# One VectorE addition in place of eight TensorE transposes in every group of a sparse attention layer

## What is computed

```
q, k, v = z @ Wq + bq, z @ Wk + bk, z @ Wv + bv
scores  = einsum('ehd,ehd->eh', q[row], k[col]) * scale + bias
p       = exp(scores - segment_max(scores, row)[row])
out     = segment_sum((p / ssum[row])[:, :, None] * v[col], row)
```

## Time and profile before

| | |
|---|---|
| time, median of 3 runs | 3586.26 us (3585.55 to 3590.37) |
| profiled execution, first to last instruction | 3582.9 us |
| PE busy | 2804.5 us (78%), 18837 instructions |
| VectorE busy | 2651.1 us (74%), 6486 instructions |
| ScalarE busy | 1708.3 us (48%) |
| GpSimd busy | 2364.8 us (66%) |
| mean granted clock of TensorE | 0.878 |

### The profile page before, as it was taken

One profiled execution on the slowest core, in us unless ns is written; L12 is line 12 of the kernel. 1 busy time (PEld: TensorE's weight loads), 2 busy tenths in 40 slices (PEclk: granted clock), 3 DMA queues, 4 the chain that ended last, 5 costly groups with the idle time before them and its releaser, 6 DMA issues.

```text
span 3582.9 us, 83361 instructions
## 1 busy us (share of the span) xinstructions
PE 2804.5 (78%) x18837; PEld 2141.8 (60%) x18838; DVE 2651.1 (74%) x6486; ACT 1708.3 (48%) x6613; POOL 2364.8 (66%) x2567
## 2 busy tenths in 40 slices
PE   8666566666656666388889988989899999999987
PEld 7433333333333333377777777778777877777775
DVE  9776676776766677377787877778777777787775
ACT  0111111111111111277777677777777767677774
POOL 0477777777777777676766666666666666666660
PEclk9877766667766677699999999999999999999999
DMA  7323322223332322777888888788788787878760
GB/s 293 84 81 84 85 77 80 75 79 79 88 81 75 82 75 72 281 286 273 293 300 302 280 298 310 275 296 301 258 295 286 275 293 269 304 271 304 245 220 24
DMA packets 287973, 719.27 MB, mean 201 GB/s; under 512 B 89203, under 2 KB 105779, under 8 KB 287686
## 3 DMA queue, kind: packets, MB, share of 16 engines
q0 software_dynamic: 214080, 585.55, 47.0%
q1 hardware_dynamic: 73862, 133.41, 11.9%
HBM read 725.41 MB, written 72.97 MB: 223 GB/s over the span
## 4 chain that ended last, share of the span: by engine, by line
PE 23%; issue 20%; POOL 19%; DVE 16%; DMA 7%; DVEq 6%; ACT 5%; ACTq 1%; POOLq 1%; SPq 0%; PEld 0%; PEldq 0%
POOL records L411 18%; PE bank L1358 9%; DMA records<-region_c,pos_i 6%; ACT region_c L731 5%; DVE region_c L1021 4%; PE wide L1417 3%; PE bank L1401 3%; PE bank L1258 2%; PE wide L1428 2%; PE wide L1376 2%; DVE region_c L1032 2%; POOL region_a L535 2%; DMA region_a<-kv,cols 1%; PE wide L1386 1%; DVEq L1056 1%
## 5 line engine op out<-in xcount | busy, mean ns | idle before, releaser
L535 POOL DMA_INDIRECT region_a<-kv,cols x1176 | 1174.0, 998 | 532.6 <-issue 454.6
L411 POOL DMA_INDIRECT records<-region_c,pos_i x1024 | 1012.7, 989 | 445.1 <-issue 410.6
L731 ACT ACTIVATE region_c<-region_a,pr 128x64 f32 x4704 | 1171.2, 336 | 33.7 <-issue 33.7
L1021 DVE TENSOR_TENSOR region_c<-region_a,bank 128x1024 f32<-128x1024 f32 x588 | 678.9, 1214 | 68.1 <-issue 48.1
L1358 PE MATMUL bank<-ident,region_c 128*128 128x128 f32 x4704 | 596.2, 281 | 115.6 <-DVE region_c L1021 112.3
L1358 PEld LDWEIGHTS bank<-ident,region_c 128*128 128x128 f32 x4704 | 568.3, 195 | 150.8 <-issue 145.6
L1376 PE MATMUL wide<-ident,region_c 128*128 128x128 f32 x4704 | 574.7, 275 | 78.7 <-ACT region_c L731 78.7
L1376 PEld LDWEIGHTS wide<-ident,region_c 128*128 128x128 f32 x4704 | 521.5, 144 | 113.0 <-ACT region_c L731 113.0
L653 ACT COPY region_c<-region_a 128x64 f32 x128 | 32.5, 254 | 1066.1 <-DMA records<-region_c,pos_i 1066.1
L1316 PE MATMUL bank<-region_b,region_a 128*128 128x512 f32 x768 | 493.6, 802 | 0.0
L1032 DVE TENSOR_TENSOR region_c<-region_a,bank 128x1024 f32<-128x1024 f32 x294 | 344.3, 1211 | 0.5 <-issue 0.5
(11 more groups left out here) (185 smaller groups left out, 3206.8 us busy)
## 6 DMA issues: line engine op xcount, KB each, us to landing
region_a<-srcT SPq DMA_DIRECT2D x128, 256.0 KB
region_a<-kv,cols POOLq DMA_INDIRECT x1176, 5.9
region_a<-hiT SPq DMA_DIRECT2D x256, 64.0 KB
records<-region_c,pos_i POOLq DMA_INDIRECT x1024
x_rows<-region_c SPq DMA_DIRECT2D x32, 512.0 KB, 3.4
kv<-region_a SPq DMA_DIRECT2D x32, 512.0 KB
records<-region_c SPq DMA_DIRECT2D x32, 480.0 KB, 14.8
region_a<-in_x_dram SPq DMA_DIRECT2D x32, 256.0 KB, 3.2
```

The costliest lines, as they stand in the source:

```text
L411: pool.indirect_dma_start(records, bass.IndirectOffsetOnAxis(ap=pos_i[j % 2][:, s:s + 1], axis=0), rec_w[j % 2][:, s, :], None).then_inc(S ...
L535: pool.indirect_dma_start(KV[r][:, s, :], None, kv, bass.IndirectOffsetOnAxis(ap=cols[r][:, s:s + 1], axis=0), bounds_check=L - 1, oob_is_ ...
L731: last = act.activation(vw[:, s, of], v_part[:, s, C + hd * D:C + (hd + 1) * D], ACT.Copy, scale=pr[:, s + 1, hd:hd + 1])
L1021: last = dve.tensor_tensor(prods[:, of, :], kv_in[:, of, 0:C], q_ps[:, :].unsqueeze(1).broadcast_to([P, 2, C]), ALU.mult)
```

## The change

VectorE weighs its pairs in the other order, slots 4-5 first, waits for its pipeline to empty (`drain`), and adds the second pair onto the first: `vw[2:4] = vw[2:4] + vw[4:6]`, 128 by 1024 floats, both inputs and the output in SBUF. A new semaphore `v_added` tells TensorE that the sum is there; `sum_v(1)` waits for it, `sum_v(2)` is dropped, and six slots are transposed and accumulated in place of eight. The slots of GpSimd's ring are still released by the two multiplications.

```diff
-                for s in range(2, GROUP - 2, 2):
-                    dve.wait_ge(SUMMED[s // 2], groups)
+                for s in (4, 2):
+                    if s == 2:
+                        dve.wait_ge(SUMMED[1], groups)
                     dve.tensor_tensor(vw[:, s:s + 2, :].rearrange("p s (h d) -> p s h d", h=HEADS),
...
                                       ALU.mult).then_inc(V_READY[s // 2], 1)
+                dve.drain()
+                dve.tensor_tensor(vw[:, 2:4, :], vw[:, 2:4, :], vw[:, 4:6, :], ALU.add).then_inc(S["v_added"], 1)
...
-                pe.wait_ge(V_READY[pair], ahead)
+                pe.wait_ge(V_IN[pair], ahead)
...
                     sum_v(1)
                     if stage == 2:
                         pe.reg_mov(coming, count_after(pe, t))
-                    sum_v(2)
                     sum_v(3)
```

More of the change, by code:

```diff
@@ L227, in layer_kernel @@
             phase1_pe weights2 q_loaded xb_ready xb_loaded cols_ready cols_free row_ready prods_a prods_b scT_ready
-            scT_sb_ready sc_summed sc_ready p_ready v_pair0 v_pair1 v_pair2 v_pair3 summed0 summed1 summed2 summed3 landed0 landed1 landed2 landed3 vT_sb_ready acc_ready acc_taken
+            scT_sb_ready sc_summed sc_ready p_ready v_pair0 v_pair1 v_pair2 v_pair3 v_added summed0 summed1 summed3 landed0 landed1 landed2 landed3 vT_sb_ready acc_ready acc_taken
             att_ready att_turned
@@ L239, in layer_kernel @@
         V_READY = [S[f"v_pair{pair}"] for pair in range(PAIRS)]
-        SUMMED = [S[f"summed{pair}"] for pair in range(PAIRS)]
+        SUMMED = {pair: S[f"summed{pair}"] for pair in (0, 1, 3)}
+        V_IN = {0: V_READY[0], 1: S["v_added"], 3: V_READY[3]}
         PRODS = [S["prods_a"], S["prods_b"]]
@@ L1002, in _ @@
             dve.reg_mov(now, 1)
-            for sem_of in ("v_pair1", "v_pair2"):
+            for sem_of in ("v_pair1", "v_pair2", "v_added"):
                 dve.sem_inc(S[sem_of], RING)
@@ L1345, in _ @@
             pe.reg_mov(ahead, RING)
-            for sem_of in ("y_taken", "y_done", "z2_turned", "acc_ready", "summed0", "summed1", "summed2", "summed3"):
+            for sem_of in ("y_taken", "y_done", "z2_turned", "acc_ready", "summed0", "summed1", "summed3"):
                 pe.sem_inc(S[sem_of], 1)
@@ L1447, in body @@
                     with pe.If(t > 0):
-                        for pair in range(PAIRS):
+                        for pair in V_IN:
                             sum_v(pair)
```

## The result

The changed kernel takes **3719.21 us** (median of 4 runs, 3718.43 to 3721.02), the kernel before 3585.91 us beside it (3584.41 to 3590.37). The ratio is **1.0372 [1.0358, 1.0385]**: slower by 133 us, where 144 were forecast.

The account below looks back on a forecast made before the run. VectorE was taken to pace a tile's last groups and stage 0, TensorE and ScalarE stages 1 to 3. Addition less slack, +131.7, and first three tiles, +12, gave +143.7 us on the span: 3730 us, range 3690 to 3780.

Parts of the forecast that it names:

- What bounds the kernel: Second phase: VectorE's pace sets a tile's last groups and stage 0 of the next, TensorE and ScalarE set stages 1 to 3.
- The addition: VectorE, every group: the added instruction with its drain costs 1.29 us, 165.1 us over the last 29 tiles.
- The slack: VectorE's true waiting in stages 2 and 3: 1.15 us a tile, 33.4 us taken off the addition's cost.
- The idle-time rival: All 110.2 us that VectorE idles before TensorE's results is usable slack: +55 us, 3641 us; chance 0.07.
- The first three tiles: Start of the second phase, 19 groups: between 0 and 24.5 us more, the middle taken, +12 us.
- The transposes: TensorE's eight dropped transposes, 0.98 us a group: nothing gained, since the last pair waits for ScalarE's slots.
- TensorE's rival: TensorE's own work decides the end of the V sum and gets shorter: -144 us, 3442 us; chance 0.04.
- The contention: Rival: the addition waits for running gathers on GpSimd, +75 us more, 3805 us; chance 0.05.
- The clock: Rival: TensorE idles longer before stage 0's products and its clock falls, unhidden, +45 us more, 3775 us; chance 0.07.

## Why the prediction was right

**What bounds the kernel: held.** That VectorE's program sets the last groups of a tile and stage 0, and TensorE and ScalarE the stretch from stage 1 to the softmax of stage 3, is shown by two things: stage 0 and the fifth group grew by the whole addition, while stages 1 to 3 together absorbed 1.3 to 1.45 us of it; and removing VectorE's work counted in the kernel before in stage 0 and the fifth group (there only by half), and not in the sum of stages 1 to 3. The border was drawn too simply. Stage 1 was counted to TensorE and ScalarE, yet it grew by the whole addition: their chain runs through it, but VectorE waits for nothing there, and the slack comes only in stages 2 and 3. The sum used the slack alone, so this cost it nothing.

**The addition, 1.29 us a group: 1.32.** The parts are visible in the rows above: the second multiplication ends at 2784.95 + 2.35 = 2787.30, the addition starts at 2787.39 (a gap of 0.09; 0.08 forecast), and the next instruction 1.14 us behind that (1.13). The 0.03 us make 128 x 0.03 = 4 us.

**The slack, 1.15 us a tile: mis-sized, 1.3 to 1.45** (5 x 1.32 - 5.31 and 4 x 1.32 - 3.83). The prediction read it from one tile, and as idle time. Both readings were a little short, as these two rows of the kernel before show, beside the earlier trace rows:

```profile
2455.82 0.23 DVE L1067 TENSOR_TENSOR sc<-bank,region_c 128x64 f32<-128x64 f32 x1 [1.34 <-PE bank L1366]
...
2747.45 0.16 DVE L1151 COPY sc<-m_run 128x8 f32<-128x8 f32 x1
```

Without a wait the scaling starts 0.07 us behind the start of that copy (2788.60 - 2788.53 in the rows of after), so its delay in stage 2 was 2748.15 - 2747.45 - 0.07 = 0.63 us, not the 0.53 of the idle time: a wait also takes away the overlap with the instruction ahead. And the tile that was read was one with little slack in stage 3: its softmax idled 1.20 us there, while the median is 1.35 in tiles of five (1.34 in the row shown) and 1.29 in tiles of four, which go from 1.20 to 1.42. With 0.59 left in after, 1.34 makes 0.75. So the tile read had 0.63 + 0.61 = 1.24 us, the tile shown 0.63 + 0.75 = 1.38; absorbed were 1.38 on average over the 28 tiles. Why tiles of five absorbed 1.29 and tiles of four 1.45 isn't settled. The term is then -29 x 1.38 = -40 us where the prediction had -33.4, the largest part of the 8.6 us by which it was too high on the span. The idle-time rival stood on the 1.44 us ahead of stage 2's softmax being slack; they are there in after too, so they were none.

**The first three tiles, +12: +9.3.** Within the bounds; the middle was a guess that no row supported, and that it came close is luck. VectorE's waits there shrank as foreseen.

**The transposes, nothing: nothing.** Shown by the run without them; a group's eight were 0.87 us of TensorE, not 0.98. TensorE's rival (3442 us) fell with that, and the idle-time rival (3641) with the periods. The sum with the measured terms is 128 x 1.32 - 40 + 9.3 = 138, against the span's 135.1; of the rest, 2.2 us lie ahead of the phase. The forecast of 3730 us was 10.8 us too high: 8.6 in the span, where the addition was 4 us too low and the slack and the first tiles too high, which partly cancels, and 2.2 because the runs' median lies 1.2 us over the span in after, not 3.4.

**The contention: the reason given was wrong, though the price was right.** The prediction says that L1130's rows say that a gather doesn't count as a reader. They show one order only, a gather that had begun 0.02 us before L1130. The trace of before held the other order as well, three times:

```profile
1735.97 0.69 DVE L1130 TENSOR_TENSOR region_c<-region_c 128x512 f32 x1 [0.56 <-issue]
...
1736.10 1.44 POOL L535 DMA_INDIRECT region_a<-kv,cols  x1 [0.30 <-issue]
```

This gather began 0.13 us after L1130 and took 1.44 us. In after it is 122 gathers that start inside an addition, 1.39 us on average, up to 2.03; 118 of them take over 1.1 us, and each of those ends 0.86 to 0.88 us behind the addition's end, however early it began; the 59 that ran already when an addition began took 0.997 us, and the 59 additions above them 1.227 us against 1.225 for the rest. So the engine that is held up is GpSimd, not VectorE, as one of them in stage 0 of a tile shows:

```profile
2802.79 2.35 DVE L1034 TENSOR_TENSOR region_c<-region_a,bank 128x1024 f32<-128x1024 f32 x2
...
2805.23 1.23 DVE L1039 TENSOR_TENSOR region_c<-region_c 128x1024 f32<-128x1024 f32 x1
2806.01 1.30 POOL L536 DMA_INDIRECT region_a<-kv,cols  x1 [5.87 <-DVE region_c L1034]
2806.37 0.69 DVE L1044 TENSOR_TENSOR wide<-wide,pr 128x512 f32<-128x512 f32 x1
```

The Trainium skill (page "SBUF — State Buffer", section "Who interferes with whom") says that a VectorE instruction with two SBUF inputs contends with a GpSimd instruction that reads SBUF, and that the second to issue is fully blocked. The trace agrees for the second being GpSimd: a gather that starts inside an addition doesn't get done until 0.86 us behind the addition's end, and with the second input in PSUM none of 118 such gathers takes over 1.1 us. For the other order it does not show the addition blocked at all: 1.227 us against 1.225. So the rival's +75 us didn't come: VectorE isn't held, and GpSimd, which is, has the time, with 636.1 us of idle time before its gathers.

**The clock: it fell, and was hidden.** The chance of 0.07 had two conditions, and one came true. Ahead of the first sums of stage 0 TensorE now idles 1.66 to 3.71 us, and in 22 of the 29 tiles the sixteen transposes behind took 2.61 to 3.65 us, in the other seven 2.04 or 2.05. The granted clock over these transposes is 0.50 to 0.74 in eight of the 22, one or both of the two levels, and 1.00 in four of the seven. The timeline at the start of such a stage:

```profile
2800.76 3.57 PE L1362 MATMUL bank<-ident,region_c 128*128 128x128 f32 x16 [2.59 <-DVE region_c L1022]
```

The engines' busy time by stretch (the third column from the end is the granted clock), first over these transposes, then over all tiles but the first three:

```profile
2800.90:2804.20 3.30, 3.30 (x17) 3.30 (x18) 3.30 (x4) 0.00 (x0) 0.00 (x0) 0.51 0.76 298
...
1730.00:3648.00 1918.00, 1557.03 (x10922) 1314.41 (x10921) 1563.04 (x2698) 1318.62 (x5198) 1205.58 (x1308) 0.97 0.76 263
```

The same view of the kernel before, over all tiles but the first three:

```profile
1723.00:3512.00 1789.00, 1612.55 (x11922) 1380.69 (x11923) 1408.80 (x2571) 1318.84 (x5197) 1162.19 (x1309) 1.00 0.80 282
```

0.51 is the level of 1.2 GHz; the sixteen transposes took 3.57 us in place of 2.04. The mean over the tiles fell from 1.00 to 0.97. But stage 0 grew by 1.32 us, the addition's cost and no more, and it is as long in the tiles where the transposes took 2.04 us (15.07 to 15.09, one 14.97) as in those where they took over 2.6 (15.06 to 15.08, one 15.16). So the fall was hidden: VectorE's weighing, scaling and weights go on meanwhile, and the softmax of that stage starts about 3 us behind the end of its scores.

## What to carry to other kernels

Before work is moved from one engine to another, find for each the stretch in which it sets the pace: the same 1.2 us of VectorE cost 1.32 in one stage and 0.5 in another, and the transposes taken from TensorE were worth nothing. To size slack, take an idle time only as far as the releaser truly ended late (compare its end with the start, in several tiles), and add the overlap that the wait took away (0.10 us here). And look between the instructions of the engine that sets the pace: register work behind a drain was 17 us of the kernel before and 76 us of the changed one.

## What I had not expected

- A gather that starts inside a VectorE instruction with two SBUF inputs ends 0.86 us behind that instruction (it takes 1.39 us on average against 0.997 us, up to 2.03), while a gather under way delays nothing. Evidence of one order is none for the other.
- Taking away the drain behind the softmax, ahead of nothing that reads its result on VectorE, gave 16 us (3569.63 to 3554.02), as much as moving the register work.
- A clock that falls in 22 of 29 tiles, for up to 3.65 us, can cost nothing, when the engine isn't the one that is waited for.
